# First attention of a two-layer transformer kernel: values stationary in four 32-column tiles, probabilities moving, in place of probability blocks stationary and 17 columns moving

## The reference, cut to what matters

```python
x = L0_attn_x                                   # [8, 256, 256] here
xn = _layernorm(x, axis=-1)
s = _L0_attn_ref(xn, L0_attn_W_qkv, L0_attn_W_o)      # softmax(q k^T + bias) v, then W_o
g = _silu(_L0_ffn_ref(xn, L0_ffn_W1, L0_ffn_W2, L0_ffn_W3))
x = x + s * g
```

## Time and profile before

| | |
|---|---|
| median of 3 runs | 1598.86 us (1597.57 to 1600.78) |
| the profiled execution's span | 1605.8 us |
| PE / ACT / DVE / POOL busy | 95% / 48% / 62% / 36% |
| first phase (8 batches) | 0 to about 516 us |
| one steady batch | 58.35 to 61.3 us |

### The profile page before, as it was taken

One profiled execution on the slowest core, in us unless ns is written; L12 is line 12 of the kernel. 1 busy time (PEld: TensorE's weight loads), 2 busy tenths in 40 slices (PEclk: granted clock), 3 DMA queues, 4 the chain that ended last, 5 costly groups with the idle time before them and its releaser, 6 DMA issues. The chain is left out here.

```text
span 1605.8 us, 26059 instructions
## 1 busy us (share of the span) xinstructions
PE 1533.6 (95%) x9424; PEld 1364.0 (85%) x9424; DVE 994.2 (62%) x1701; ACT 771.0 (48%) x1623; POOL 570.6 (36%) x502
## 2 busy tenths in 40 slices
PE   5899999999999999999999999999899999999997
PEld 4688889889888789999989998999878888888885
DVE  7454654654654676767666766666556666666666
ACT  4354554554454445545445554455434444444443
POOL 3323432432422334444434444444322232233322
PEclk8699998998897999999999999999999999999998
DMA  4200000000000300000000000000001000001001
GB/s 145 79 13 3 13 13 0 13 13 0 13 13 24 122 27 1 27 1 28 1 28 1 27 1 25 1 24 1 1 29 41 23 23 23 23 23 46 0 1 53
DMA packets 16200, 37.88 MB, mean 24 GB/s; under 512 B 2036, under 2 KB 10868, under 8 KB 14710
## 3 DMA queue, kind: packets, MB, share of 16 engines
q1 hardware_dynamic: 16120, 36.76, 6.6%
HBM read 30.46 MB, written 6.29 MB: 23 GB/s over the span
## 5 line engine op out<-in xcount | busy, mean ns | idle before, releaser
L1698 POOL TENSOR_TENSOR z1l<-z,z1h 128x512 fp32r<-128x512 f32 x96 | 128.1, 1335 | 300.5 <-ACT z1h L1095 300.5
L1664 POOL TENSOR_TENSOR rstd<-msq,half_pow 128x8 f32<-128x8 f32 x64 | 104.7, 1636 | 212.1 <-DVE msq L1411 212.1
L991 ACT ACTIVATE pT<-trio,rstd 128x256 f32<-128x256 f32 x128 | 60.8, 475 | 194.8 <-PE trio L617 194.8
L1133 DVE TENSOR_TENSOR yT1l<-trio,yT1h 128x512 fp32r<-128x512 f32 x64 | 44.3, 692 | 150.0 <-ACT yT1h L1044 150.0
L1676 POOL TENSOR_TENSOR pT<-pT,tri_mul 128x512 f32<-128x512 f32 x64 | 81.8, 1278 | 155.6 <-ACT pT L1039 155.6
L1612 POOL TENSOR_TENSOR hid_l<-hid,hid_h 128x256 fp32r<-128x256 f32 x64 | 47.5, 741 | 248.3 <-ACT hid_h L853 246.1
L1522 DVE TENSOR_TENSOR u<-bank,h 128x512 f32<-128x512 f32 x88 | 60.9, 692 | 118.9 <-ACT h L1086 118.9
L1404 DVE TENSOR_TENSOR sq<-xs 128x512 f32<-128x512 f32 x128 | 109.3, 854 | 31.8 <-ACT xs L1004 31.7
L578 PE MATMUL bank<-bw_h,xT1h 128*128 128x512 f32 x256 | 108.8, 425 | 8.8 <-issue 5.8
L1095 ACT ACTIVATE z1h<-z 128x512 fp32r<-128x512 f32 x96 | 60.8, 633 | 116.3 <-DVE z L1539 100.9
L580 PE MATMUL bank<-bw_l,xT1h 128*128 128x512 f32 x256 | 102.9, 402 | 0.0
(11 more groups left out here) (234 smaller groups left out, 5202.9 us busy)
## 6 DMA issues: line engine op xcount, KB each, us to landing
raw<-pack_moe_dram SPq DMA_DIRECT2D x12, 896.0 KB, 4.5
raw<-pack_attn_dram SPq DMA_DIRECT2D x8, 1024.0 KB, 5.0
raw<-pack_w_dram SPq DMA_DIRECT2D x2, 1024.0 KB, 4.8
xT_scratch<-xT1h_c SPq DMA_DIRECT2D x8, 256.0 KB, 2.1
xT_scratch<-xT1l_c SPq DMA_DIRECT2D x8, 256.0 KB, 2.2
xT1h<-xT_scratch SPq DMA_DIRECT2D x8, 256.0 KB, 4.6
xT1l<-xT_scratch SPq DMA_DIRECT2D x8, 256.0 KB, 5.3
out_dram<-x_all SPq DMA_DIRECT2D x8, 256.0 KB, 2.1
```

Of the source, the lines that this page charges most:

```text
L1664: pool.tensor_tensor(out=rstd[:, r, :], in0=msq[:, r, :], in1=half_pow[:], op=ALU.pow).then_inc(rstd_sb, 1)
L1698: pool.tensor_tensor(out=z1l[:, r, :], in0=z1[:, r, :], in1=z1h[:, r, :].bitcast(F32), op=ALU.subtract).then_inc(z1l_sb, 1)
```

## The change: what it does

`mix` swaps the operands. A head's values, padded from 17 to 32 columns (`VW`), are stationary and its probabilities move. Four heads go to the four 32-column tiles of the array and write partitions 0 to 31, 32 to 63, and so on. Per head there is one matmul of 256 columns (both query tiles against key tile 0) and one of 128 (key tile 1), so 8 per group. The result now has heads and channels on the partitions, so ACT copies it to the new buffer `yt0` (`heads_T`), PE transposes it back with two 128 x 128 transposes (`heads_back`), and DVE's `heads_out` reads that. Group 3 gets a bank of its own (`more`, bank 1). `heads_T` stands in the middle of `exps` of the next group on ACT. `scores(b, 2)` now stands ahead of `logits_T`. The batch's end changes too: `out_T` is moved to the next batch, to the place where `project_out` stood, and `project_out` goes behind `queries_keys(b, 1)`, into another bank. Two router buffers are laid over a weight buffer that is free by then.

```diff
             def mix(b, g):
-                n = MIX_BANK[g]
                 pe.wait_ge(pT0_sb, 12 * b + 3 * g + 3)
...
-                o = banks[n][:, 0:TT * GH * (E0 + 1)].rearrange("p (t h e) -> p t h e", t=TT, h=GH)
+                o = [MIX_BANK[g][h * VW:(h + 1) * VW, 0:T] for h in range(GH)]
                 for h in range(GH):
-                    hh = g * GH + h
-                    pe.matmul(o[:, 0, h, :], pT0[:, 0, h, :], v0[:, 0, hh, :], start=True, stop=True)
-                    pe.matmul(o[:, 1, h, :], pT0[:, 1, h, :], v0[:, 0, hh, :], start=True, stop=False)
-                    last = pe.matmul(o[:, 1, h, :], pT0[:, 2, h, :], v0[:, 1, hh, :], start=False, stop=True)
+                    pe.matmul(o[h], v0[:, 0, g * GH + h, :], pT0[:, 0:2, h, :], start=True, stop=False)
+                for h in range(GH):
+                    last = pe.matmul(o[h][:, P:T], v0[:, 1, g * GH + h, :], pT0[:, 2, h, :], start=False, stop=True)
                 last.then_inc(y0_ps, 1)
+
+            def heads_back(b, g):
+                pe.wait_ge(yt0_sb, 4 * b + g + 1)
+                for tt in range(TT):
+                    last = pe.transpose(MIX_BANK[g][:, T + tt * P:T + (tt + 1) * P], yt0[:, tt * P:(tt + 1) * P], ident[:])
+                last.then_inc(yq0_ps, 1)
...
                 queries_keys(b, 0)
                 if not first:
-                    project_out(t)
+                    out_T(t)
                 pe.wait_ge(qT0l_sb, 2 * b + 1)
                 queries_keys(b, 1)
-                after(pe, s0_sb, b)
+                if not first:
+                    project_out(t)
...
                 down(b, 6)
-                pe.wait_ge(hid_sb, 8 * b + 8)
                 mix(b, 3)
                 down(b, 7)
-                if not final:
-                    pe.wait_ge(xT0l_sb, b + 2)
-                out_T(b)
+                heads_back(b, 3)
...
+            def heads_T(b, g):
+                act.wait_ge(y0_ps, 4 * b + g + 1)
+                act.activation(yt0[:], MIX_BANK[g][:, 0:T], ACT.Copy).then_inc(yt0_sb, 1)
...
-                exps(b, 2)
+                exps(b, 2, (0,))
+                heads_T(b, 1)
+                exps(b, 2, (1,))
...
-                exps(b, 3)
+                exps(b, 3, (0,))
+                heads_T(b, 2)
+                exps(b, 3, (1,))
```

More of the change, by code:

```diff
@@ L36 @@
 GR = GH * E0
+VW = P // GH
 KR = GR + 2
@@ L115, in build @@
         r_th, r_sc = sa("r_th", [P, TT, NE]), sa("r_sc", [P, TT, NE])
-        r_gt, r_ge = sa("r_gt", [P, TT, NE, NE]), sa("r_ge", [P, TT, NE, NE])
+        r_gt, r_ge = (w2_a[:, n * TT * NE * NE:(n + 1) * TT * NE * NE].rearrange("p (t i j) -> p t i j", t=TT, i=NE)
+                      for n in range(2))
         r_rank, r_w = sa("r_rank", [P, TT, NE]), sa("r_w", [P, TT, NE])
@@ L216, in build @@
         UP_BANK = (1, 0, 1, 1, 1, 1, 0, 1)
-        MIX_BANK = (0, 0, 1, 1)
+        MIX_BANK = (banks[0][:, :], banks[0][:, :], banks[1][:, :], more[:, 1, :])
         hadamard, tri_add32 = y0[:, 0, 0:P], y0[:, 0, P:2 * P]
@@ L485, in batch @@
                 scores(b, 1)
+                after(pe, s0_sb, b)
                 probs_T(b, 0, (0, 1))
@@ L515, in batch @@
                     up(b, 4)
+                    heads_back(b, 0)
+                scores(b, 2)
                 pe.wait_ge(y0_sb, 4 * b + 1)
@@ L822, in queries_keys, with exps @@
                 act.activation(kT0h[0:GR, 2 * pair:2 * pair + 2, :], kT0[0:GR, :, :], ACT.Copy).then_inc(kT0h_sb, 1)
-            def exps(b, g):
+            def exps(b, g, tiles=range(TT)):
                 act.wait_ge(max0, 8 * b + 2 * g + 2)
-                for t in range(TT):
+                for t in tiles:
                     for h in range(GH):
@@ L833, in exps, with out_T @@
                         last = act.activation(o, i, ACT.Exp, bias=nmax[:, g, t, h:h + 1])
-                last.then_inc(exp0, 1)
+                if t == TT - 1:
+                    last.then_inc(exp0, 1)
+            def heads_T(b, g):
+                act.wait_ge(y0_ps, 4 * b + g + 1)
+                act.activation(yt0[:], MIX_BANK[g][:, 0:T], ACT.Copy).then_inc(yt0_sb, 1)
+            def out_T(b):
+                act.wait_ge(yT0_ps, b + 1)
+                act.activation(yT0h[:].rearrange("p k t -> p (k t)"), banks[0][:, :], ACT.Copy).then_inc(yT0h_sb, 1)
             def probs_T(b, g, blocks):
@@ L882, in project_out @@
                 after(act, x1_sb, b)
-                act.activation(s0[:].rearrange("p t d -> p (t d)"), banks[0][:, :], ACT.Copy).then_inc(s0_sb, 1)
+                act.activation(s0[:].rearrange("p t d -> p (t d)"), more[:, 0, :], ACT.Copy).then_inc(s0_sb, 1)
             def ffn_hi(n, w):
@@ L922, in batch @@
                     norm_T1(t)
-                exps(b, 1)
+                if first:
+                    exps(b, 1)
+                else:
+                    exps(b, 1, (0,))
+                    heads_T(b, 0)
+                    exps(b, 1, (1,))
                 if first:
@@ L960, in batch @@
                 hidden_hi(b, 7)
-                act.wait_ge(yT0_ps, b + 1)
-                act.activation(yT0h[:].rearrange("p k t -> p (k t)"), banks[0][:, :], ACT.Copy).then_inc(yT0h_sb, 1)
+                heads_T(b, 3)
             norm_T0(0)
@@ L1220, in heads_out, with out_T @@
                    .then_inc(y0_sb, 1)
+            def out_T(b):
+                dve.wait_ge(yT0h_sb, b + 1)
+                lo(yT0l[:].rearrange("p k t -> p (k t)"), banks[0][:, :], yT0h[:].rearrange("p k t -> p (k t)"))\
+                    .then_inc(yT0l_sb, 1)
             def gate_out(b):
@@ L1259, in router @@
                     other, own = r_sc[:].unsqueeze(2).to_broadcast(four), r_sc[:].unsqueeze(3).to_broadcast(four)
-                    link(dve.tensor_tensor(out=r_ge[:], in0=other, in1=own, op=ALU.is_ge))
-                    link(dve.tensor_tensor(out=r_ge[:], in0=r_ge[:], in1=before[:].unsqueeze(1).to_broadcast(four),
+                    link(dve.tensor_tensor(out=r_ge, in0=other, in1=own, op=ALU.is_ge))
+                    link(dve.tensor_tensor(out=r_ge, in0=r_ge, in1=before[:].unsqueeze(1).to_broadcast(four),
                                            op=ALU.mult))
-                    link(dve.tensor_tensor(out=r_gt[:], in0=other, in1=own, op=ALU.is_gt))
-                    link(dve.tensor_tensor(out=r_gt[:], in0=r_gt[:], in1=r_ge[:], op=ALU.max))
+                    link(dve.tensor_tensor(out=r_gt, in0=other, in1=own, op=ALU.is_gt))
+                    link(dve.tensor_tensor(out=r_gt, in0=r_gt, in1=r_ge, op=ALU.max))
                 if 1 in parts:
-                    link(dve.tensor_reduce(out=r_rank[:], in_=r_gt[:], axis=AX.X, op=ALU.add))
+                    link(dve.tensor_reduce(out=r_rank[:], in_=r_gt, axis=AX.X, op=ALU.add))
                     link(dve.scalar_tensor_tensor(out=r_w[:], in0=r_rank[:], scalar=float(TOPK), in1=r_sc[:],
```

25 lines of the change are left out of this document (15 added, 10 removed).

## The result

The changed kernel took 1622.68 us (median of 4 runs, 1621.86 to 1627.07) against 1598.51 us for the kernel before beside it; the ratio is 1.0138, 95% interval [1.0112, 1.0165]. It is 24 us slower where 19 us faster was forecast, and outside the range. The profiled execution took 1622.40 us, at the median, and spans 1620.6 us. That is 14.8 above the span of before, which itself stands 6.9 us above the median of its runs; so the difference of the two spans is smaller than that of the medians.

A forecast was written before the change was run, and what follows sets the result against it. PE, busy 95% of the span, was taken to set the pace. +2 us for seven batches, +1 for the first and -22 for the clock made -19: from 1598.9 to 1580 us, 8-in-10 range 1558 to 1608.

The forecast's parts named there:

- Group 0: Mix of group 0 to scores(b, 2): PE waits 0.5 us for exponentials behind the copy; net -0.5 us per batch.
- signs of being wrong: Mean clock staying at 0.91, mix over 2.2 us, or a full-clock batch over 1 us from 55.4 us.
- The clock term: PE's low clock behind 17-column mixes, 118 to 516 us: two thirds of the loss comes back, 22 us.
- The mix's price: A group's new mix on PE takes 1.5 us instead of 2.70, with 0.65 and 2.6 us as the ends.
- Rival C: In the mix, column tiles do not overlap, so it stays at 2.6 us; 1607 us in total, chance 0.20.
- Group 1: Mix 1 to scores(b, 3): PE waits some 1.2 us for exponentials behind the copy, losing the saving; net 0.
- Group 2: Behind mix 2: the router holds back group 3's exponentials, so the mix's saving becomes idle time; net +0.4 us per batch.
- Batch start: Group 3's mix and the next batch's start: PE waits 1.6 us on qT0l, 1.0 us on yT0l; net +0.4 us.
- First batch: In the first batch, DVE's heads_out waits behind ACT's weight copy, ahead of the Hadamard's low part: +1 us.

The follow-up runs named there:

- e4: The changed kernel with 36 unused filler matmuls on PE behind group 0's transposes, where PE waits for POOL's keys; 1595.44 us, ratio 0.9934 to the kernel before.
- e10: The kernel before with 64 moving columns in its mix instead of 17, and hid_h of block 2 ahead of group 1's exponentials on ACT; 1567.10 us, ratio 0.9762.
- e8: The changed kernel with only ACT's hid_h of block 2 moved ahead of the exponentials of group 1; 1560.14 us, ratio 0.9721 to the kernel before.
- e2: The changed kernel with group 0's heads_T behind all eight exponentials and hid_h of block 2 ahead of group 1's exponentials on ACT; 1560.36 us, ratio 0.9719.
- e11: e2 with DVE's yT0l ahead of kz0h and the maxima of group 3 between the router's two parts; 1534.38 us, ratio 0.9553 to the kernel before.
- e6: e2 with out_T back at the batch's end and project_out between the two queries_keys; 1562.55 us, ratio 0.9746 to the kernel before.
- e3: The kernel before with only ACT's hid_h of block 2 moved ahead of the exponentials of group 1; 1588.37 us, ratio 0.9911.
- e9: The kernel before with 64 moving columns in its mix instead of 17, the extra products unused; 1584.61 us, ratio 0.9876.

## Why the prediction was wrong

**The step that failed** is "Group 0": that PE, behind the new mix, "waits 0.5 us" for the exponentials and nets -0.5 us. It waits 5.2 us, for POOL. I had followed ACT's new order to the exponentials (forecast to end 3.7 us behind the mix's start; they end 2.75 us behind it, as the mix is shorter) and had not asked what stands on ACT behind them and who waits for that: `hid_h`, hence POOL's whole queue. The trace of before held it. POOL, and then PE:

```profile
299.92 0.72 POOL L1612 TENSOR_TENSOR hid_l<-hid,hid_h 128x256 fp32r<-128x256 f32 x1 [6.65 <-ACT hid_h L853]
300.81 1.89 POOL L1604 TENSOR_TENSOR kz0h<-kT0h,head_mask 64x1024 fp32r<-64x1024 f32 x1 [0.17 <-POOL hid_l L1612]
302.66 1.89 POOL L1604 TENSOR_TENSOR kz0l<-kT0l,head_mask 64x1024 fp32r<-64x1024 f32 x1
```

```profile
304.60 0.39 PE L347 MATMUL trio<-tri_add,ident_b 128*128 128x512 bf16 x1
```

POOL's keys ended at 304.55 us and the scores started at 304.60: no slack at all. The slow mix, the logits and the low clock filled PE's time up to that moment. The 5.2 us of wait add up from both sides: 1.9 us saved in the mix, 0.9 us because the feed-forward block behind it now runs at 2.4 GHz (1.5 us in place of 2.4), 1.3 us of logits moved behind the scores, 1.3 us by which the scores' start comes later counted from the mix (7.9 us in place of 6.6), less 0.2 us for the transposes. A saving ahead of a fixed arrival is no saving.

**What the total says.** Per steady batch 55.7 us at full clock and 1.6 us of remaining loss to the clock were forecast, 57.3 us; 63.1 were measured. e4 splits the 5.8 us between them: its 59.2 us at 0.99 are 58.7 at full clock, 3.0 us above the forecast's 55.7, and the other 2.8 us are the clock. Times seven this is 41 of the 43 us between 1580 and 1622.7. Two of the prediction's own signs of being wrong came true: the mean clock stayed at 0.91, and a batch at full clock is over 1 us from 55.4.

**The clock term** had the right cause and the wrong balance. A microsecond at 1.2 GHz costs about 0.46 us (e10 against before: 28.4 us for 61 us of low level, some 2 us of it shorter waits; forecast 0.45). The falls behind the old mix went away. But the wait took their place: 72 us of low level over six batches, where I had taken two thirds of the loss as coming back (22 us) and had no case in which it grows. Some 3 us per batch of that low level lie within the wait itself (303 to 308 has a clock of 0.69) and cost nothing. The clock came back in e8 (10 us of low level) and e4 (7 us). So the mean of 0.91 in both kernels has two different causes.

**The mix's price** was off to the good side, 0.79 against 1.5 us: I had let the two passes of one head follow each other and hold up the next head. The Trainium skill's "up to 4×" for a small dimension of at most 32 ("TensorEngine Tiling (Array Packing)", Overview, Theoretical Speedup) agrees with the trace, 2.70 / 0.79 = 3.4. The Trainium skill's sentence that weight loads overlap with matmuls in flight only when the row groups differ ("TensorE: Matmul & The Clock Gate", Part 3) does not hold for these column tiles, which share all rows. The matmuls of group 1, batch 4, and their weight loads:

```profile
318.14 0.64 PE L374 MATMUL bank<-pT,v 128*32 128x256 f32 x8
318.60 0.40 PE L376 MATMUL bank<-pT,v 128*32 128x128 f32 x8
```

```profile
318.14 0.16 PEld L374 LDWEIGHTS bank<-pT,v 128*32 128x32 f32 x8 [0.18 <-ACT pT L862]
318.38 0.34 PEld L376 LDWEIGHTS bank<-pT,v 128*32 128x32 f32 x8
```

Each of the 16 loads lasts 0.11 us, yet eight are over in 0.16 us: loads into different column tiles overlap each other. And the loads of L376 begin at 318.38, 0.22 us ahead of its first matmul, while those of L374 are in flight. With the full array the rows of before hinted at it, which I had missed: loads fill 85% of the span and matmuls 95%. Rival C falls.

**The other parts**, once POOL's wait is gone. Batch 4 has no low level in it, neither in e2 nor in e10, so its sections can be compared with the forecast's net terms at full clock:

| section, us | e10, old mix | e2, new mix | net | forecast |
|---|---|---|---|---|
| mix 0 to scores 2, with 0.7 us of logits moved out | 4.94 | 2.57 | -1.7 | -0.5 |
| mix 1 to scores 3 | 3.74 | 2.93 | -0.8 | 0 |
| mix 2 to mix 3 | 7.90 | 8.65 | +0.8 | +0.4 |
| mix 3 to the next scores 0 | 11.31 | 11.21 | -0.1 | +0.4 |

The batch is 1.9 us shorter in e2 (53.5 against 55.4) where 0.3 us longer was forecast, mostly because the mix is 0.7 us cheaper than assumed. In the kernel after the first section is 7.9 us, +3.6 net.

**Group 1** held in its direction: PE waits for the exponentials behind the copy, but 0.7 us and not 1.2. **Group 2** held: the exponentials of group 3 stay behind the router. PE waits 1.3 us there for the returned copy (1.4 forecast) and 0.9 us more for the exponentials; e11 shows what this was worth. **Batch start**: the wait on `qT0l` is 1.6 us as forecast, that on `yT0l` 0.6 and not 1.0. With a mix 0.7 us cheaper than assumed the section nets -0.1 and not +0.4, so the terms for the moved start, +1.4 in the forecast, were about right against the kernel before; that e6 finds nothing to win back has another reason, the late heads. **First batch**: forecast 1 us longer, it came out 7 us shorter. The clock accounts for nearly all of it: up to mix 0 of batch 1 the profile of before has 41 us of low level and takes 118.4 us, those of after, e3, e9 and e10 have 27 us and take 111.3 to 112.3. Since e3, e9 and e10 have the old mix, it is no effect of the new one; whether before differs from them there by its code or in this one execution, no run shows.

## What to carry to other kernels

When a block on the bottleneck engine gets shorter, list every semaphore that the work behind it waits for and read when each of them arrived before; the one that arrived "just in time" becomes the wait. Where an instruction with a new wait goes into an in-order queue, follow what stands behind it to the end, through other engines' queues: here a copy of 0.38 us and the wait in front of it held back POOL's keys, two queues away, by 1.2 us. And idle time or thin passes on PE cost twice, in themselves and in the clock that follows.

## What the runs showed of the hardware

- Four 32-column tiles with fp32 operands: four matmuls with 256 moving columns and four with 128 (16 passes) in 0.79 us; full overlap of the streams alone would be 0.65 us, an estimate from the earlier trace rows.
- An fp32 pass with 17, 64 or 128 moving columns and 128 stationary ones takes the same time, 0.11 us, yet the clock fell far more often with the 17-column form than with the 64-column form (61 against 14 us of low level over six batches; with `hid_h` early 44 against 0).
- Work without use in a wait of 5 us gave 33 us of 1620 back (e4), through the clock: the time behind the wait, not the wait, got shorter.
